# Two batches shifted by half a layer: placing one batch's feed-forward and next projection inside the other's attention

## The reference, cut to what matters

```python
def _layer(x, wqkv, qs, ksc, wo, lg, lb, w1, b1, w2, b2):
    h = shift_token(x)                     # upper 64 columns come from the token before
    q, k, v = split(h @ wqkv, 3)           # 128 -> 3 x 512, 8 heads of 64
    q = l2norm(q) * qs
    k = l2norm(k) * ksc
    q, k = rotary_xpos(q, k)
    o = local_attention(q, k, v)           # windows of 64 tokens, each sees itself and the one before
    x = x + o @ wo
    h = shift_token(x)
    h = (h - mean) / sqrt(var + 1e-05) * lg + lb
    a, g = split(h @ w1 + b1, 2)           # 128 -> 2 x 341
    return x + (a * gelu(g)) @ w2 + b2
```

## Time and profile before

| | us |
|---|---|
| median of 3 runs | 814.53 |
| lowest to highest | 814.22 to 815.98 |
| profiled execution, its own time | 814.73 |
| span of that execution in the profile | 812.9 |
| stage D in it (516.5 to 812.9) | 296.4 |

### The profile page before, as it was taken

The page is one execution under the profiler, slowest core; times in us unless marked ns, Lnnn a source line. Parts: engine busy times, 40 slices in busy tenths (PEclk is TensorE's granted clock), DMA queues, the critical chain, the costliest instruction groups (busy, mean ns, idle before and its releaser), DMA issues.

```text
span 812.9 us, 13454 instructions
## 1 busy us (share of the span) xinstructions
PE 643.8 (79%) x4866; PEld 397.2 (49%) x4866; DVE 570.6 (70%) x1187; ACT 500.1 (62%) x1205; POOL 234.2 (29%) x229
## 2 busy tenths in 40 slices
PE   7579985876889989958989787756788697488866
PEld 3222232453456656635555455524576463367555
DVE  7882328547999989577777775499745559984565
ACT  4469978643778868424576576464556449355742
POOL 5030022010988969841000000002633000063500
PEclk8879987878555555565799999886698999659998
DMA  9400000000000000000000000000000000000000
GB/s 300 154 1 1 2 1 0 0 1 0 1 2 2 1 1 1 1 1 0 1 2 1 1 2 1 0 1 1 1 2 2 1 0 1 1 2 2 2 1 26
DMA packets 9062, 10.58 MB, mean 13 GB/s; under 512 B 2747, under 2 KB 7845, under 8 KB 8869
## 3 DMA queue, kind: packets, MB, share of 16 engines
q1 hardware_dynamic: 8996, 9.73, 3.7%
HBM read 9.21 MB, written 0.52 MB: 12 GB/s over the span
## 4 chain that ended last, share of the span: by engine, by line
PE 43%; DVE 33%; ACT 11%; issue 8%; POOL 3%; DMA 1%; ACTq 0%; DVEq 0%; POOLq 0%
PE ps L1401 5%; PE ps L1661 4%; DVE s_nmB L1049 4%; PE ps L1564 4%; PE ps L1644 3%; ACT arena L536 3%; PE ps L1681 2%; PE ps L1472 2%; PE ps L1551 2%; PE ps L1748 2%; PE ps L1756 2%; PE ps L1853 2%; PE ps L1444 2%; PE ps L1389 2%; ACT dev L665 2%
## 5 line engine op out<-in xcount | busy, mean ns | idle before, releaser
L385 POOL TENSOR_SCALAR arena<-arena,s_rB,s_zpu 128x512 uint8<-128x512 f32 x128 | 115.9, 943 | 42.6 <-DVE s_rB L1022 41.3
L574 ACT ACTIVATE arena<-ps,s_nmB 128x512 f32<-128x512 f32 x128 | 86.6, 683 | 31.8 <-DVE s_nmB L1049 31.2
L596 ACT ACTIVATE arena<-ps,s_nmx 128x512 f32<-128x512 f32 (+3 forms) x128 | 60.7, 527 | 49.7 <-DVE s_nmx L1147 49.2
L1049 DVE TENSOR_REDUCE s_nmB<-ps 128x2 f32<-128x1024 f32 x64 | 77.3, 1217 | 6.9 <-PE ps L1551 6.6
L420 POOL COPY arena<-arena 64x512 f32<-64x512 f32 x16 | 12.6, 790 | 240.7 <-PE ps L1748 238.9
L1142 DVE TENSOR_REDUCE s_nmx<-ps 128x1 f32<-128x512 f32 (+3 forms) x128 | 56.6, 483 | 20.5 <-PE ps L1647 20.1
L536 ACT ACTIVATE arena<-ps 128x1024 f32<-128x1024 f32 x64 | 60.9, 1026 | 6.5 <-PE ps L1456 6.5
L1564 PE MATMUL ps<-cst,arena 128*128 128x128 f32 x256 | 61.9, 422 | 1.2 <-ACT arena L566 0.8
L1407 PE MATMUL ps<-ones 128*128 128x512 f16 x134 | 44.1, 493 | 22.7 <-ACT s_wn L507 6.6
L1564 PEld LDWEIGHTS ps<-cst,arena 128*128 128x128 f32 x256 | 49.3, 221 | 14.4 <-POOL arena L385 7.9
L1551 PE MATMUL ps<-staged 8*128 8x512 f16 x128 | 46.6, 585 | 11.8 <-ACT arena L574 10.9
(11 more groups left out here) (346 smaller groups left out, 1567.0 us busy)
## 6 DMA issues: line engine op xcount, KB each, us to landing
vec<-in_vec SPq DMA_DIRECT2D x1, 1882.0 KB, 11.9
w_d<-in_wqkv SPq DMA_DIRECT2D x2, 768.0 KB
vec<-in_vec SPq DMA_DIRECT2D x1, 960.0 KB, 8.1
w_h<-in_w SPq DMA_DIRECT2D x2, 341.0 KB
x_tok<-in_x SPq DMA_DIRECT2D x1, 512.0 KB, 4.1
arena<-in_w_f SPq DMA_DIRECT2D x2, 256.0 KB, 7.8
rope<-in_rope SPq DMA_DIRECT2D x1, 512.0 KB, 10.5
w_do<-in_wo SPq DMA_DIRECT2D x2, 256.0 KB
```

The lines of the kernel that those rows point to most:

```text
L385: nc.gpsimd.tensor_scalar(u8[:, n % 4, j // 2, :, 2 * (j % 2)], prob[:, n % 2, j * 512:j * 512 + 512], sm("rB", 8)[:, c:c + 1], sm("zpu", ...
L574: nc.scalar.activation(prob[:, n % 2, j * 512:j * 512 + 512], ps[:, j, :], ACT.Exp, bias=sm("nmB", 8)[:, c:c + 1], accum_out=sm("sumB", 8) ...
L596: nc.scalar.activation(probC[:, n % 2, at(qt):at(qt) + w], ps[:, bank, col:col + w], ACT.Exp, bias=nmx[:, TB * b + qt, h:h + 1]).then_inc( ...
L1049: free(V.tensor_reduce(sm("nmB", 8)[:, c:c + 2], ps[:, 2 * half:2 * half + 2, :], X, ALU.max, negate=True), "maxB")
```

## The change: what it does, and the diff

The layer loop goes. Stage D becomes four rounds; round n is the attention of batch n mod 2 in layer n div 2. What a batch does after its attention is cut into eleven parts (E_PARTS), what it does ahead of the next attention into fifteen (F_PARTS). Round n holds, at fixed places between its units, the E parts of the attention just finished (round n - 1, the other batch) and then the F parts that lead to the next round's attention (n + 1, the other batch again). Each step of a round has three places: ahead of the scores, of the maximum and of the exponentials (place 0); after them (place 1); and ahead of the product with the values (place 2). A part stands in the same place in the lists of PE, ACT and DVE. Rounds 1 and 2 take three parts per step, round 0 (F parts only) two, round 3 (E parts only) one. F parts of round 0 stand ahead of the loop, E parts of round 3 behind it.

Attention now keeps banks 0 to 3: one buffer for the scores (0 and 1), one for the transposed probabilities (2), one for the outputs (3). The parts share banks 4 to 7: the projection has one set of three banks. The feed-forward keeps its data in the batch's own part of `qkvD`, and each step of it is done on four tiles at a time (one gelu, one gate, one sum). ACT now does all evacuations of q and k.

```diff
+        ROUNDS = B * DEPTH
+        UNITS = 2 * TB
+        E_PARTS = ("project", "shift", "spread", "normal", "turn_e", "hid0", "hid1", "gelu", "gated", "turn_g", "add")
+        F_PARTS = ("turn_f", "proj0", "proj1", "proj2", "proj3", "norms", "rope0", "rope1", "rope2", "rope3", "rope4",
+                   "rope5", "rope6", "turn0", "turn1")
+        PER_STEP = (2, 3, 3, 1)
+        def part_at(n, u, place):
+            parts = [(p, n - 1) for p in E_PARTS] if n else []
+            if n + 1 < ROUNDS:
+                parts += [(p, n + 1) for p in F_PARTS]
+            per = PER_STEP[n]
+            k = per * u + place - (1 if per < 3 else 0)
...
-            return ps[:, 6 * (u % 2):6 * (u % 2) + 2, 0:256].rearrange("p j (a k) -> p j a k", k=P)
+        scores_d = ps[:, 0:2, 0:256].rearrange("p j (a k) -> p j a k", k=P)
```

ACT, in each round (left out are the four exponentials):

```diff
+                for u in range(UNITS + 3):
+                    U = UNITS * n + u
+                    part_d(*part_at(n, u, 0))
+                    if u < UNITS:
+                        act.wait_ge(sem["maxD"], U + 1)
...
+                    part_d(*part_at(n, u, 1))
+                    if 2 <= u < UNITS + 2:
+                        act.wait_ge(sem["ptD"], U - 1)
...
+                        nc.scalar.activation(probTD[:, u % 2, :], ps[:, 2, :], ACT.Copy).then_inc(sem["ptcD"], 1)
+                    part_d(*part_at(n, u, 2))
```

ACT, some of the parts:

```diff
+                if name in ("proj0", "proj1", "proj2", "proj3"):
+                    act.wait_ge(sem["d_mm"], TB * m + tt + 1)
+                    nc.scalar.activation(qkvD[:, t, :], ps[:, 4:7, :].rearrange("p a b -> p (a b)"), ACT.Copy)\
+                        .then_inc(sem["d_ev"], 1)
...
+                    nc.scalar.activation(sqD, qkvD[:, t, 0:2 * INNER], ACT.Square).then_inc(sem["d_sq"], 1)
+                if name == "norms":
...
+                    load_table(ACT.Exp)
+                if name == "spread":
+                    act.wait_ge(sem["lnvar"], m + 1)
+                    nc.scalar.activation(sm("std")[:, r], sm("var")[:, r], ACT.Sqrt).then_inc(sem["lnstd"], 1)
+                    load_table(ACT.Exp if m + 1 < ROUNDS else ACT.Gelu)
+                if name == "gelu":
+                    act.wait_ge(sem["e_ev"], TB * (m + 1))
+                    g = hidD[b][:, :, HID:2 * HID]
+                    nc.scalar.activation(g, g, ACT.Gelu).then_inc(sem["gelu"], 1)
+                    if m + 1 < ROUNDS:
+                        load_table(ACT.Exp)
```

DVE, in each round (left out are the maximum with its product, and the reciprocal of the sums of unit u - 1):

```diff
+                    part_d(*part_at(n, u, 0))
+                    if u < UNITS:
+                        dve.wait_ge(sem["sD"], U + 1)
...
+                    if u >= 5 and u % 2:
+                        put_o(n, (u - 5) // 2)
+                    part_d(*part_at(n, u, 1))
+                    if 1 <= u <= UNITS:
+                        dve.wait_ge(sem["expD"], 4 * U)
...
+                    part_d(*part_at(n, u, 2))
```

PE, in each round (left out are the four transposes of unit u - 2, and the product with the values of unit u - 3):

```diff
+                    part_d(*part_at(n, u, 0))
...
+                    if u < UNITS:
+                        if U:
+                            pe.wait_ge(sem["expD"], 4 * U)
+                        s_d(b, u)
+                    part_d(*part_at(n, u, 1))
+                    if 2 <= u < UNITS + 2:
+                        pe.wait_ge(sem["normD"], U - 1)
...
+                    part_d(*part_at(n, u, 2))
+                    if u >= 3:
...
```

More of the change, by code:

```diff
@@ L276, in evacuate_qk @@
+        PER_STEP = (2, 3, 3, 1)
[5 more added lines that the diff above has]
+            k = per * u + place - (1 if per < 3 else 0)
+            if place < (1 if per < 3 else 0) or place - (1 if per < 3 else 0) >= per or k >= len(parts):
+                return (None, 0)
+            return parts[k]
         def evacuate_qk(copy, b, i):
[L278 removed]
+            return copy((qTD, kTD)[i // 4][:, i % 4, b * 512:b * 512 + 512], ps[:, 4 + i % 4, :])
@@ L344, in _ @@
                 sp.wait_ge(sem["result"], b + 1)
-                load(out[b].rearrange("(t p) c -> p t c", p=P), wide["dev"][:, TB * b:TB * b + TB, :], "stored")
+                load(out[b].rearrange("(t p) c -> p t c", p=P), wide["x1"][:, TB * b:TB * b + TB, :], "stored")
             sp.wait_ge(sem["stored"], 16 * B)
@@ L700, in _ @@
+            for name in E_PARTS:
+                part_d(name, ROUNDS - 1)
         @block.vector
@@ new lines, in part_d @@
+                if name == "gated":
+                    dve.wait_ge(sem["gelu"], m + 1)
+                    free(V.tensor_tensor(hgD[b], hidD[b][:, :, 0:HID], hidD[b][:, :, HID:2 * HID], ALU.mult), "hg")
+                    if l + 1 < DEPTH:
+                        step(V.memset(uT[64:P, 512 * b:512 * b + 1], 0.0), "constants")
+                if name == "add":
+                    dve.wait_ge(sem["g_mm"], m + 1)
+                    add(f[:, r, :], f[:, r, :], ps[:, 7, :].rearrange("p (t c) -> p t c", t=TB))
+                    add(f[:, r, :], f[:, r, :], per_tile(v_("b2")[:, l * D:(l + 1) * D], TB), "f_ready")
+                    if l + 1 == DEPTH:
+                        add(h[:, r, :], f[:, r, :], x[:, r, :], "result")
@@ new lines, in pv_d @@
+            def pv_d(t, v):
+                for half in range(2):
+                    rows = slice(0, WINDOW if half == 0 and t % TB == 0 else P)
+                    for a in range(2):
+                        for j in range(2):
+                            pair, c = 2 * (v % 2) + a, P * (2 * j + a) + WINDOW * half
+                            values = 2 * INNER * half + DHD * (2 * pair + j)
+                            o = P * pair + WINDOW * half
+                            ins = M(ps[64 * j:64 * j + 64, 3, o:o + WINDOW], qkvD[rows, t, values:values + DHD],
+                                    probTD[rows, v % 2, c:c + WINDOW], start=True, stop=True)
+                ins.then_inc(sem["pvD"], 1)
```

695 lines of the change are left out of this document (288 added, 407 removed).

## The result

The changed kernel takes 902.92 us (median of 4 runs, 900.86 to 904.42) against 814.99 us for the kernel before in the same comparison. The ratio is 1.1077, 95% interval 1.1051 to 1.1102: 88 us slower. The forecast was 897 us, range 855 to 930.

The account below looks back on a forecast made before the run. No engine is full, so waits between engines count. Warm terms 42 + 57 + 86 + 86 + 51 + 35 = 357 us for stage D against 296.4, plus 22 for the clock, led to 897 us; range 855 to 930.

Parts of the forecast that it names:

- head: Start of stage D, one batch's projection, rotation, factors and transposes before the first scores: 42 us against 40.2 before.
- tail: End of stage D, the last batch's output projection, feed-forward and store with nothing beside them: 35 us warm.
- the clock's term: Stage D, extra for PE running below its 2.4 GHz clock: 6 us per full round, 22 in all.
- The chain of a full round: Rounds 1 and 2, step by step between last output copies: 86 us warm for half a layer, against 73.5 before.
- steps 1 and 2: Full round, normalisation and first feed-forward tiles: score matmuls of the later step start about 14 us after the earlier's.
- Scaled widths: Wide feed-forward operations, durations scaled from nearest rows: bias add 0.85 us, gelu 1.35, gate 1.6.
- the cold bound: Stage D with every PE piece on the chain at the low clock: 25 us more per full round, 86 in all.
- the warm sum of 357: All pieces of stage D added with the clock at 2.4 GHz: 357 us against 296.4 before.
- Table loads: Stage D, ACT function tables: about 21 loads against 11, each priced at 1.28 us without a drain.
- Cold almost throughout (961): Rival for stage D: all chain pieces on PE at half clock, 961 us in all; chance 0.10.
- The faster one: Rival: lists run past each other, each round costs its busiest engine's work, 780 us; chance 0.06.
- The smaller loss (845): Rival: table loads, feed-forward copies and half of steps 6 and 7 hide, 15 us less per full round; chance 0.06.

Follow-up runs that it names:

- e2_behind: Changed kernel with place 0 moved behind the scores, maximum and exponentials of its step: 903.13 us, ratio 1.109.
- e11_less_parts: Changed kernel with the rotation of k left out of every projection, its scaling kept: 876.81 us, ratio 1.0747.
- e3_no_tables: Changed kernel with stage D's square roots and gelu replaced by copies of the same size, so only the first exponential table loads there: 894.15 us, ratio 1.0979.
- e1_serial: Changed kernel with all parts of a round placed ahead of its first unit, on all three engines: 1007.85 us, ratio 1.2377.
- e12_less_attention: Changed kernel leaving out all but the last of the eight products with the values in every unit: 903.78 us, ratio 1.1111.
- e7_warm: Changed kernel with 12 extra unread matmuls, twice in rounds 1 and 2 and in the tail (layer norm, gelu): 899.33 us, ratio 1.1049.
- e9_warm_close: Changed kernel with e7_warm's extra matmuls and more right ahead of the waits before the feed-forward and the gated rows' turn: 888.48 us, ratio 1.0939.
- e4_one_buffer_before: Kernel before with one PSUM buffer each for scores, transposed probabilities and outputs: 857.38 us, ratio 1.0536.

## Why the prediction was right

The sum held by its terms, nearly all of them a little small. The pieces of stage D in us, forecast with the clock and measured: head 42 and 45.7, round 0 60 and 63.7, round 1 92 and 92.6, round 2 92 and 89.6, round 3 55 and 53.7, tail 38 and 39.9. The forecast of 379 for the stage stands against 385. That it came so near rests in part on luck: the clock's term could by its own bounds have been anything from 0 to 86 us.

**The chain of a full round.** Right in its pieces and nearly in length. From the start of round 1 the chain of waits reaches the end of the feed-forward's sum after 41.4 us (forecast 37.95, warm), the last copy of the projection after 60.9 (56.65), the last scaling of k after 84.5 (79.1) and the last output copy after 92.6 (86): the 6 us for the clock fill the difference. The masks ahead of the scores of steps 1 and 2 stand 14.3 us apart, where I had 14, and those of steps 2 and 3 10.8 (forecast 10); timeline of PE:

```profile
634.89 0.39 PE L1683 MATMUL ps<-dmask,identb 128*128 128x256 bf16 x2 [1.81 <-ACT sq L678]
649.23 0.38 PE L1683 MATMUL ps<-dmask,identb 128*128 128x256 bf16 x2
660.07 0.63 PE L1683 MATMUL ps<-dmask,identb 128*128 128x256 bf16 x2
```

**The reason I gave for it** was half wrong. I wrote that a part in place 0 holds back the maximum, the exponentials and the unit after them. They are held back, but it costs nothing: moving place 0 gave nothing back (e2_behind). The greater part of a round is one batch's own line of work, output projection to rotated q and k, 81 us alone, with 18 us of the other batch's attention on the same chain. My chain had the same pieces on it, so its length was right; but I read it as attention delayed by parts, and in the full rounds it is better read as parts delayed by attention. Of attention's 41 us, 29 are hidden. Leaving out 31 us of rotation work gave 27 (e11_less_parts), which fits either reading; that a shorter softmax would give back no more than its share of the chain is not shown.

**Scaled widths**, from the groups by shape of stage D after (count, busy, mean ns of one, idle before); forecast 0.85, 1.6 and 1.35 us:

```profile
L1299 DVE TENSOR_TENSOR arena<-ps,vec 128x682 f32<-128x682 f32 x16 | 13.9, 869 | 21.3 <-PE ps L1775 21.3
...
L1303 DVE TENSOR_TENSOR arena<-arena 128x1364 f32<-128x1364 f32 x4 | 6.3, 1580 | 14.3 <-ACT arena L654 14.3
...
L654 ACT ACTIVATE arena<-arena 128x1364 f32<-128x1364 f32 x4 | 5.4, 1342 | 8.1 <-DVE arena L1299 8.1
```

**Head, round 0 and tail** were under-sized, with the clock, by 3.7, 3.7 and 1.9 us. The head had no term for the clock at all. Its first projection tile took 4.51 us (granted clock 0.64) and the others 2.84, where the row gave 2.64 for tiles that follow each other without a wait. In the tail the feed-forward matmuls took 7.1 us where I had 4 x 1.31, and the output projection 5.4 where I had 3.84; the row of cold tiles would have said so, and I put it into the clock's term instead.

**The clock.** I took a quarter of the cold bound, 22 us. The stage is 28 over the warm sum of 357, and the second run with extra matmuls shows some 11 of it. A quarter was a choice and not a derivation. PE's own work in a full round, 50 us by my chain, was 59. The windows of round 1 (feed-forward, projection, rotation) show both levels in turn, the projection near 2.4 GHz as I had it, and rotation, which I had not counted, lowest:

```profile
625.40:660.00 34.60, 19.95 (x134) 15.27 (x135) 13.68 (x28) 15.43 (x37) 3.29 (x4) 0.70 0.00 0
660.00:690.00 30.00, 23.53 (x213) 14.46 (x215) 15.93 (x26) 19.14 (x39) 4.40 (x5) 0.95 0.01 1
690.00:718.00 28.00, 15.75 (x170) 13.34 (x162) 20.00 (x27) 13.19 (x33) 8.01 (x7) 0.63 0.00 1
```

**Table loads.** 21 in the stage, as forecast, and no idle time ahead of them in which a drain could stand. I had some 14 of them on the chain; there are 11, 13.6 us, and leaving all out gave 8 to 9 (e3_no_tables).

**The rivals.** Cold almost throughout (961) fell: the stage's clock is 0.77. The faster one fell at its own point: a full round takes 92.6 against the 55.7 from which it decides. The smaller loss (845) fell too: some table loads do hide, but a full round is not 15 us shorter than the chain. Of the signs, PE's busy sum in the stage (242.4) lies in the 210 to 250 forecast, the tail with 39.9 just outside its 35 to 38. The rule it leaned on (the Trainium skill, "Perfetto Trace Analysis", "Optimization Strategy") is not refuted: interleaving is worth 105 us against none (e1_serial). But the kernel before already overlapped both batches tile by tile, with two sets of buffers, and the new interleaving replaces that one.

**Open.** How the 88 us split. The PSUM split costs 48 us in the old order; whether it costs as much in the new one could only be tried with more PSUM than there is. The other 40 or so, the one batch's line and the unshared head and tail, are the difference and not a measurement. Parts and attention as the two sides of a full round were not parted by a clean pair of runs.

## What to carry to other kernels

Before two items are shifted against each other, lay out the longest line that one item must go through within a round, with nothing beside it. If that alone (here 81 us) is longer than the stage takes per item now (73.5), placing the other item's work well is not enough to win; the line itself would have to get shorter. Count what the shift gives up: each unit of attention that had two PSUM buffers and gets one turns into maximum, exponentials, scores in strict turn, here 44 us in the old order. And a busy sum says nothing on which of two interleaved lists decides; take work out of each in turn, in like amounts, and from what each of them waits for.

## What the runs showed of the hardware

- PE work beside the chain was nearly free: 112 matmul records less in each round changed the four by -1.6, +1.0, +2.7 and -3.3 us (e12_less_attention).
- Extra matmuls kept the clock up only where they reached to the critical ones: with 3 us of idling between, the feed-forward took 6.53 us (e7_warm), without it 5.00 (e9_warm_close).
- The same three projection matmuls take 2.64 us a tile in a row of tiles and 2.84, at a granted clock of 1.00, where each tile waits for the copy of the last.
- The one-buffer chain of a unit took 3.9 us at the upper level of the clock and 4.6 to 4.7 at a mean of 0.59 (e4_one_buffer_before), though scores to maximum are only 1.1 us of it.
